# Scans and experts interleaved in one unrolled block, with the scan's operands split between SBUF and PSUM

## The reference

```python
x  = L0_attn_x
xn = layernorm(x)
# scan part, D = 256 channels, N = 16 states, over 2048 steps of each of 2 rows
delta = softplus(xn @ W_delta.T + delta_bias)
B_sel, C_sel = xn @ W_B.T, xn @ W_C.T            # each (b, l, D, N)
A_bar = exp(delta[..., None] * A)
h = A_bar * h + (A_bar - 1.0) / A * B_t * x_t    # step by step
y = sum(h * C_t, axis=-1)
# expert part, E = 8 experts, top 2 of them, hidden width 1024
scores = xn @ Wr + br
w = softmax(where(top2 mask, scores, -inf))
out = sum_e w[e] * (gelu(xn @ W1[e] + b1[e]) @ W2[e] + b2[e])
x = x + y + out
```

## Time and profile before

| what | us |
|---|---|
| median of 3 runs | 1458.48 (1458.33 to 1459.33) |
| span of the profiled execution | 1459.1 |
| VectorE, TensorE, GpSimd, ScalarE busy | 1122.0, 1220.7, 870.4, 593.4 |
| first scan stage, from GpSimd's first operation | from 98.3 |
| expert stage, starts of its first and last matmul | 564.6 to 996.3 |
| second scan stage begins | 998.3 |
| last VectorE operation ends | 1455.7 |

### The profile page before, as it was taken

The page is one execution under the profiler, slowest core; times in us unless marked ns, Lnnn a source line. Parts: engine busy times, 40 slices in busy tenths (PEclk is TensorE's granted clock), DMA queues, the critical chain, the costliest instruction groups (busy, mean ns, idle before and its releaser), DMA issues. The chain is left out here.

```text
span 1459.1 us, 23731 instructions
## 1 busy us (share of the span) xinstructions
PE 1220.7 (84%) x7674; PEld 727.2 (50%) x7674; DVE 1122.0 (77%) x1357; ACT 593.4 (41%) x1128; POOL 870.4 (60%) x582
## 2 busy tenths in 40 slices
PE   1668888878879776999999999999888878888775
PEld 0533333333333324899989999995333333333332
DVE  6869999999999995334334334336999999999998
ACT  3735425425434533444444444443532532532331
POOL 3639979979988983010010010015978978988975
PEclk9569999999999998999999999999999999999998
DMA  6672312321321325777777777762102101101100
GB/s 208 220 243 80 133 70 83 112 93 53 137 97 47 112 101 182 257 244 256 257 243 258 257 243 258 257 200 89 40 15 61 36 18 58 40 18 54 37 11 30
DMA packets 89546, 189.84 MB, mean 130 GB/s; under 512 B 13249, under 2 KB 63937, under 8 KB 79521
## 3 DMA queue, kind: packets, MB, share of 16 engines
q1 hardware_dynamic: 75872, 126.56, 26.2%
q0 software_dynamic: 13632, 62.80, 13.2%
HBM read 139.52 MB, written 49.81 MB: 130 GB/s over the span
## 5 line engine op out<-in xcount | busy, mean ns | idle before, releaser
L783 POOL TENSOR_TENSOR uxb<-ub,x 128x512 f32<-128x512 f32 x256 | 466.9, 1825 | 100.3 <-DVE ub L861 97.1
L934 PE MATMUL bank<-k_xT,k_WC 128*128 (+1 forms) x1536 | 388.2, 390 | 150.8 <-DVE hcb L878 130.3
L869 DVE TENSOR_TENSOR_SCAN hb<-aexp,state,uxb 128x512 f32<-128x512 f32 x256 | 417.0, 1629 | 25.4 <-POOL uxb L783 25.4
L934 PE MATMUL bank<-k_xT,k_WB 128*128 (+1 forms) x1536 | 388.2, 391 | 10.3 <-DVEq L849 10.0
L934 PEld LDWEIGHTS bank<-k_xT,k_WC 128*128 128x128 f16 x1536 | 139.1, 99 | 382.8 <-DVE hcb L878 207.0
L691 ACT ACTIVATE state<-hb 128x1 f32<-128x1 f32 x256 | 51.7, 202 | 553.7 <-DVE hb L869 553.7
L934 PEld LDWEIGHTS bank<-k_xT,k_WB 128*128 128x128 f16 x1536 | 153.9, 101 | 203.7 <-issue 21.4
L1062 POOL DMA_DIRECT2D w<-wsplit x39 | 20.9, 537 | 381.0 <-DVE yo L1192 372.5
L1102 PE MATMUL bank<-xbt,k_xT 128*128 128x256 f16 x1872 | 213.0, 274 | 2.7 <-ACT xbt L1148 2.7
L1117 PE MATMUL bank<-w,hs 128*128 128x256 f16 x1872 | 210.6, 273 | 0.0
L1102 PEld LDWEIGHTS bank<-xbt,k_xT 128*128 128x128 f16 x1872 | 184.2, 98 | 25.4 <-issue 1.8
(11 more groups left out here) (121 smaller groups left out, 759.3 us busy)
## 6 DMA issues: line engine op xcount, KB each, us to landing
k_xT<-wsplit SPq DMA_DIRECT2D x39, 1024.0 KB, 4.9
w<-wsplit POOLq DMA_DIRECT2D x39, 1024.0 KB, 5.4
k_yall<-in_W SPq DMA_DIRECT2D x32, 512.0 KB, 4.3
wsplit<-k_yall SPq DMA_DIRECT2D x32, 512.0 KB, 3.2
xs<-k_yall SPq DMA_DIRECT2D x1, 9984.0 KB, 32.1
k_yall<-xs SPq DMA_DIRECT2D x39, 256.0 KB, 4.8
ys<-yo SPq DMA_DIRECT2D x39, 256.0 KB, 2.2
b<-in_b POOLq DMA_DIRECT2D x39, 128.0 KB, 5.4
```

What stands on the lines that cost most here:

```text
L783: nc.gpsimd.tensor_tensor(uxb[:, s % 2], ub[:, s % 2], x32[:, hf], ALU.mult).then_inc(ux_done, 1)
L869: v.tensor_tensor_scan(hb[:, s % AR], aexp[:, s % AR], uxb[:, s % 2], state[:, s:s + 1], ALU.mult, ALU.add).then_inc(h_done, 1)
L934: ins = mm(bank[:], W[:, a, kc, n, hf * P:(hf + 1) * P], chunk(xT, c)[:, b, kc, :], start=(k == 1), stop=(k == 3 * KC))
```

## The change

Stages 2 to 4 become one block, `scan_and_experts`, whose queues are written out tile by tile for all 256 tiles (`g`), without loops. An expert block starts at every fourth tile from tile 74 (`E0`, `STEP`). In tile g each engine does its scan work first and then what is due of the experts.

- Weight pieces: one in every two tiles, tiles 0 to 66; scatters: one a tile, tiles 0 to 63.
- The scan's operands: ScalarE makes `em1` = A_bar - 1 (`less_one`, ring of 2), GpSimd multiplies it by x (`times_x`, into `ax`, ring of 2), VectorE multiplies the B bank by `ax` in place in PSUM (`ux_op`), and the scan reads `aexp` from SBUF and the B bank. `hc_op` writes into the C bank in place and `acc_op` adds it to `ysum` in SBUF. B has 3 banks, C has 2, the hidden values have 2, and one bank (`Sps`) is shared by `turn`, `down`, z and the row transposes, in the order of the list `USE`. `aexp` has 6 buffers, `hb` 3.
- The high half of the hidden values goes from VectorE to ScalarE (`high_h`), the low half from VectorE to GpSimd (`low_h`). w1 and w2 have one buffer each, and both are loaded by SyncE.
- x and the scan are added into `base` and stored to `mid` in DRAM; from tile 233 (`F0`) on GpSimd gathers three expert rows per tile, and VectorE weights and adds them (`add_expert`) to rows read back from `mid`.

```diff
-def scan_phase(nc, io, keep, banks, ctx, row):
+TILE_N = NCH * TILES
+E0 = 74
+STEP = 4
+F0 = E0 + STEP * NBLK + 3
+def block_at(g, shift):
+    b, r = divmod(g - E0 - shift, STEP)
+    return b if r == 0 and 0 <= b < NBLK else None
+def turn_block(g):
+    return 0 if g == E0 - 1 else block_at(g, 1 - STEP) if g > E0 else None
+def down_block(g):
+    return block_at(g, 2 + STEP)
+def scan_and_experts(nc, io, keep, banks, ctx):
+    AR, ER, XR, HR, BR, CR = 6, 2, 2, 3, 3, 2
+    LEAD = AR - 1
+    Bps, Cps, Hps, Sps = banks[0:3], banks[3:5], banks[5:7], banks[7]
...
+        def less_one(g):
+            act.wait_ge(a_ready, g + 1)
+            if g >= ER:
+                act.wait_ge(ax_done, g - ER + 1)
+            nc.scalar.activation(em1[:, g % ER], aexp[:, g % AR], ACT.Copy, bias=-1.0).then_inc(em1_done, 1)
...
+        def take_x(b):
+            act.wait_ge(shared_made, USE["turn", b] + 1)
...
+        for g in range(TILE_N):
+            c, s = divmod(g, TILES)
+            if g + LEAD < TILE_N:
+                exp_tile(g + LEAD)
+            if g + LEAD - 1 < TILE_N:
+                less_one(g + LEAD - 1)
+            if g >= 1 and (g - 1) // TILES % RCH != RCH - 1:
+                save_state(g - 1)
+            if g < 2 * SPLITS:
+                if g % 2 == 0:
+                    scale_piece(g // 2)
+                else:
+                    high_piece(g // 2)
+            if g >= 1 and z_part(g - 1) is not None:
+                take_z(*z_part(g - 1))
+                if z_part(g - 1)[1] == KC - 1:
+                    softplus(c + 1)
+            if g >= 1 and turn_block(g - 1) is not None:
+                take_x(turn_block(g - 1))
+            b = block_at(g, 0)
+            if b is not None:
+                gelus(b)
+                for q in range(2):
+                    high_h(b, q)
...
+        def low_h(b, q):
+            fs = slice(q * (FC // 2), (q + 1) * (FC // 2))
+            pool.wait_ge(hi_done, b * 2 + q + 1)
...
+        for g in range(TILE_N):
+            c, s = divmod(g, TILES)
+            times_x(g)
...
+            if g >= 3 and g % 2 == 1 and (g - 3) // 2 < SPLITS:
+                low_piece((g - 3) // 2)
...
+            b = block_at(g, 3)
+            if b is not None:
+                for q in range(2):
+                    low_h(b, q)
...
+        def ux_op(g):
+            bank = Bps[g % BR][:]
+            dve.wait_ge(ax_done, g + 1)
+            dve.wait_ge(B_ready, g + 1)
+            v.tensor_tensor(bank, ax[:, g % XR], bank, ALU.mult).then_inc(ux_done, 1)
...
+            v.tensor_tensor_scan(hb[:, g % HR], aexp[:, g % AR], Bps[g % BR][:],
+                                 0.0 if first else state[:, s:s + 1], ALU.mult, ALU.add).then_inc(h_done, 1)
...
+        def project_b(g):
+            if g >= BR:
+                pe.wait_ge(h_done, g - BR + 1)
...
+        def project_c(g):
+            if g >= CR:
+                pe.wait_ge(c_taken, g - CR + 1)
...
+                if fc % 2 == 0 and (b or fc >= 4):
+
+                    pe.wait_ge(gelu_done, b * FC + fc - 2)
...
+        def down(b):
+            pe.wait_ge(w2_in, (b + 1) * 32)
+            pe.wait_ge(lo_done, b * 2 + 2)
+            shared_free(("down", b))
...
+        project_b(0)
+        for g in range(TILE_N):
+            if g + 1 < TILE_N:
+                project_b(g + 1)
+            project_c(g)
+            if block_at(g, 0) is not None:
+                hidden(block_at(g, 0))
+            if turn_block(g) is not None:
+                turn(turn_block(g))
+            if down_block(g) is not None:
+                down(down_block(g))
+            if row_part(g) is not None:
+                turn_rows(*row_part(g))
+            if z_part(g) is not None:
+                project_z(*z_part(g))
```

More of the change, by code:

```diff
@@ new lines, in row_part, with shared_bank_uses @@
+def row_part(g):
+    c, s = divmod(g, TILES)
+    return (c - 1, (s - 5) // 4) if s in (5, 9) and c >= 1 else None
+def shared_bank_uses():
+    order = []
+    for g in range(TILE_N):
+        if turn_block(g) is not None:
+            order.append(("turn", turn_block(g)))
+        if down_block(g) is not None:
+            order.append(("down", down_block(g)))
+        if row_part(g) is not None:
+            order.append(("row",) + row_part(g))
+        if z_part(g) is not None:
+            order.append(("z",) + z_part(g))
+    order += [("row", NCH - 1, 0), ("row", NCH - 1, 1)]
+    return {name: i for i, name in enumerate(order)}
@@ L590, in scan_phase @@
[L590 to L616, removed]
@@ L632, in _ @@
     def _(sp):
[L633 to L664, removed]
@@ L747, in _, with save_state @@
-        for s in range(AHEAD):
-            exp_tile(0, s)
-        chunks(act, body)
+        def less_one(g):
[3 more added lines that the diff above has]
+            nc.scalar.activation(em1[:, g % ER], aexp[:, g % AR], ACT.Copy, bias=-1.0).then_inc(em1_done, 1)
+        def save_state(g):
+            act.wait_ge(h_done, g + 1)
+            s = g % TILES
+            nc.scalar.activation(state[:, s:s + 1], hb[:, g % HR, CH - 1:CH], ACT.Copy).then_inc(state_saved, 1)
@@ new lines, in gelus @@
+        def gelus(b):
+            act.wait_ge(w1_in, (b + 1) * 32)
+            for fc in range(FC):
+                if fc % 2 == 0:
+                    act.wait_ge(H_done, b * PAIRS + fc // 2 + 1)
+                if fc % (FC // 2) == 0 and b >= 1:
+                    act.wait_ge(lo_done, (b - 1) * 2 + fc // (FC // 2) + 1)
+                nc.scalar.activation(h32[:, fc, :], Hps[fc // 2 % 2][:, fc % 2 * BT:(fc % 2 + 1) * BT],
+                                     ACT.Gelu_apprx_tanh, bias=b1[:, b % 2, fc:fc + 1],
+                                     scale=1.0 / WSCALE).then_inc(gelu_done, 1)
@@ new lines, in high_h @@
+        def high_h(b, q):
+            act.wait_ge(gelu_done, b * FC + (q + 1) * (FC // 2))
+            if b >= 2:
+                act.wait_ge(shared_made, USE["down", b - 2] + 1)
+            fs = slice(q * (FC // 2), (q + 1) * (FC // 2))
+            nc.scalar.activation(hs[b % 2][:, 0, fs, :], h32[:, fs, :], ACT.Copy).then_inc(hi_done, 1)
+        act.wait_ge(keep["zeros_out"], 16)
+        for g in range(LEAD):
+            exp_tile(g)
+        for g in range(LEAD - 1):
+            less_one(g)
@@ new lines, in gather @@
+        def gather(i, j):
+            q, k = j // 2, j % 2
+            if j == 0:
+                if i == 0:
+                    for par in range(2):
+                        pool.wait_ge(y_out[par], (NBLK + 1 - par) // 2 * 16)
+                if i >= 2:
+                    pool.wait_ge(row_added, (i - 1) * 2 * CT)
+            t = i * CT + q
+            nc.gpsimd.indirect_dma_start(
+                out=gat[:, i % 2, q, k, :], out_offset=None, in_=io["ys"],
+                in_offset=bass.IndirectOffsetOnAxis(keep["slot"][:, k, t:t + 1], 0)).then_inc(gathered[i % 2], 16)
@@ new lines, in _ @@
+        pool.wait_ge(keep["zeros_out"], 16)
+        restore_x(0, 0)
+        for g in range(TILE_N):
+            c, s = divmod(g, TILES)
+            times_x(g)
+            if s == 2:
+                add_delta(c, 1)
+            if s == 5:
+                restore_x(c, 1)
+            if s == 22 and c + 1 < NCH:
+                add_delta(c + 1, 0)
+            if s == 23 and c + 1 < NCH:
+                restore_x(c + 1, 0)
+            if g >= 3 and g % 2 == 1 and (g - 3) // 2 < SPLITS:
+                low_piece((g - 3) // 2)
+            if g < 2 * NT:
+                i, k = g // 2, g % 2
+                nc.gpsimd.indirect_dma_start(
+                    out=io["xs"], out_offset=bass.IndirectOffsetOnAxis(keep["slot"][:, k, i:i + 1], 0),
+                    in_=keep["rows"][:, i].rearrange("p a d -> p (a d)"), in_offset=None).then_inc(scattered, 16)
+            b = block_at(g, 3)
+            if b is not None:
+                for q in range(2):
+                    low_h(b, q)
+            part = finish_part(g)
+            if part is not None:
+                for j in range(part[1] * 3, min(part[1] * 3 + 3, 2 * CT)):
+                    gather(part[0], j)
@@ L846, in _ @@
+        for g in range(TILE_N, F0 + 3 * NCH):
+            part = finish_part(g)
+            for j in range(part[1] * 3, min(part[1] * 3 + 3, 2 * CT)):
+                gather(part[0], j)
     @block.vector
@@ new lines, in hc_op @@
+        def hc_op(g):
+            c, hf, n = tile(g)
+            bank = Cps[g % CR][:]
+            dve.wait_ge(C_ready, g + 1)
+            dve.wait_ge(h_done, g + 1)
+            if n == 0 and c >= 2:
+                dve.wait_ge(shared_made, USE["row", c - 2, 1] + 1)
+            dst, done = (ysum[:, c % 2, hf], c_taken) if n == 0 else (bank, hc_done)
+            v.scalar_tensor_tensor(dst, hb[:, g % HR], keep["rA"][:, hf, n:n + 1], bank, ALU.mult,
+                                   ALU.mult).then_inc(done, 1)
@@ new lines, in _ @@
+        ux_op(0)
+        for g in range(TILE_N):
```

(30 more changed lines are left out.)

813 lines of the change are left out of this document (333 added, 480 removed).

## The result

| | before | after |
|---|---|---|
| median | 1458.5 us (1458.33 to 1459.33) | 1714.26 us (1713.2 to 1714.64) |
| ratio | 1 | 1.1744, 95% interval 1.1727 to 1.1761 |
| span of the profiled execution | 1459.1 us | 1711.5 us |
| granted TensorE clock, mean | 0.951 | 0.898 |

A forecast was written before the change was run, and what follows sets the result against it. It took a loop of waits between queues to bound the blocks: 442 us to the first, 17.8 for block 0, 37 x 27.5, 22 for the last, 16 to the gathers, 142 for the end: 1658 us, range 1480 to 1715.

The forecast's parts named there:

- this very case: Main case: waits between queues, not TensorE's work alone, set a block's period of 27.5 us; 1658 us in all, chance 0.68.
- The loop: In each block, down waits for the xbt copy, behind a minus-one, a GpSimd product and two low halves: 3.6 us.
- the walk: One block of four tiles followed through all queues; C(g+4) can start only at 26.15 us, the period before extras and clock.
- The stall inside hidden: In each block, hidden's pair 2 waits for the first two gelus, with two H banks: TensorE stands 1.2 us.
- The start: Tiles before the first block: 8.86 us for two tiles, 1.8 of it waiting; first block at 442 us.
- The clock: Lower TensorE clock after pauses: 0.7 us a block taken, from between 0 and 3; 10 us in the first stage.
- The end: Gathers from 1516 us, rounds of 17.7 us for three tiles as gathers await additions; 142 us to the finish.
- The TensorE-bound case: Rival: TensorE never waits in a block, whose period is its work, 21.75 us; 1445 us in all, chance 0.10.
- Only the copy's wait is absent: Rival: in the blocks, gelu stall and accumulate wait remain, period 22.8 us; 1484 us in all, chance 0.12.
- The contended port: Rival: a scan with a PSUM operand still excludes GpSimd, lengthening products and low halves; 1781 us, chance 0.10.
- The drain beside a table load: On ScalarE, about 1.38 us beside each table load, some 2 us a block, 75 us in all; left out of the sum.

The follow-up runs named there:

- the first experiment: Against the changed kernel, ScalarE's copy of xbt moved to the very start of tile g+1, before that tile's exp; 1504.2 us.

## Why the prediction was right, and where its size was off

The mechanism was right. That the time lies in the stated range is partly luck: 1714.3 us is 0.7 below its upper end of 1715, and above the 1580 to 1710 that was given for this very case.

- *The loop.* It was the main case, and it stood in the trace with the predicted members and length: pause 3.57 us on average (3.6 predicted), low halves 4.24 for two (4.24), two table loads a block. Breaking it at the copy, at the ring, or at the low halves shortened the pause to 0, 2.0 and 2.0 us, with 2.1 to 2.2 expected for the last two. One step of the walk didn't occur: C(g+4) was to wait for VectorE until 26.15, and in the blocks no projection waits for ysum. It was worth 0.15 us only, since TensorE's own queue brings C(g+4) to 26.0.
- *The stall inside hidden.* 1.1 us (1.2), removed by one early gelu.
- *The start.* The first hidden was put at 443.3 us, and it is at 443.4. In the quiet pairs of tiles GpSimd's wait for a piece's high half is 1.84 us (1.8 predicted) and the low halves start 8.9 apart (8.86); the mean of 2.13 (68.2 in 32) comes from two waits of 7.4 where a chunk's z and softplus fall. Whether the 10 us put down there for the clock are right, no run shows by itself.
- *The clock.* This is the term that was mis-sized: "between 0 and 3 us a block, I take 0.7, by the nearer full-clock rows". Down shows 6.82 - 5.13 = 1.69, and filling the pause gives back 1.73 a block. The error of 1.0 in 37 blocks is 37 of the 53 us by which the sum (1658) falls short of the span (1711.5). The reasoning that dense work around a pause would shelter it was wrong: behind 3.6 us 36 of 37 downs run partly at the lower level, behind 2.0 us 15 of 37 (ring of four) and 14 of 37 (low halves on VectorE).
- *The end.* From the last hidden's first matmul (1528.4 - 6.3) to the end it is 189.4 us, with 178.9 in the sum: 10 of the 53. A gather has a gap of 0.30 us behind another gather, so 1.25, not 1.17; and the additions, which read two SBUF tensors, stretch beside GpSimd (three took 2.98 us at 1600.56 while GpSimd issued a gather and made a product, and 1.26 at 1606.48 with GpSimd idle; median of one 0.47). The remaining 6 us lie in the blocks: block 0 took 19.6 instead of 17.8, the rest wasn't followed.
- *The rivals.* The TensorE-bound case didn't occur in the changed kernel, and did occur, at 22.1 us a block, once the queues were mended. "Only the copy's wait is absent" is nearly what the first experiment made: 1504 measured, 1484 by the rival's arithmetic, plus its share of the terms above. The contended port didn't occur with the operand in PSUM; with the operand back in SBUF it gave 1818, where the rival had 1781.
- *The drain beside a table load*, which the Trainium skill (ScalarE: Activation LUTs, section "What ACT_TABLE_LOAD costs") has and I left out after the earlier trace rows: at 863.53 the first gelu starts 0.02 us behind the load's end here too, and so does the activation behind 90 of the 92 loads of the changed kernel.

## What to carry to other kernels

When queues are merged, adding up each engine's work isn't enough: follow one period through every queue in order, and ask for each short instruction that releases another engine what it stands behind. Here a 1 us copy stood behind a ring's wait and cost 14%. Put what another engine waits for first in a tile, and what only keeps a ring full last. Price a pause of TensorE at more than its length: here 3.57 us of pause took another 1.73 from the matmuls behind it. And judge a change by its parts: the operand split was a gain of 104 us inside a change that lost 256.

## What the hardware showed that I had not expected

- Filling a pause with useless matmuls makes the kernel faster, by 64 us. After a pause of 2.0 us (ring of four) a down takes either 5.13 or 6.79 us from first to last start and nothing in between (15 of 37 the longer); after 3.6 us 28 of 37 take 6.4 to 6.8, eight take 7.7 to 8.0, and one 5.13.
- A scan whose initial value is a constant takes 1212 ns (64 times, spread 1210 to 1216), one that takes it from a column of SBUF 1273 (192 times).
- The issue of a scatter takes 1010 ns (median of 64, maximum 1187) with the scan reading one operand from PSUM; before, some took 1995, and with both operands in SBUF again the mean is 1361, against 1013, and the maximum 1769.
